# First expert stage with its weight parts, ranks and counts in other places, and attention's output projection as three products of high and low parts

## What is computed

```python
x = x + 0.5 * _L0_ffn_ref(_layernorm(x), gate_up_proj, down_proj, router_w)
x = x + _L0_attn_ref(_layernorm(x), conv_w, conv_b, wq, bq, ..., wo, bo, proj_w, proj_b)
x = x + 0.5 * _L0_ffn_ref(_layernorm(x), gate_up_proj, down_proj, router_w)
```

```python
out = mha_out @ proj_w + proj_b      # proj_w is 64 x 256
```

## Time and profile before

| | us |
|---|---|
| median of 3 runs | 794.87 |
| lowest and highest | 792.56 and 800.15 |
| the profiled execution's own time | 796.36 |
| its span in the trace | 794.6 |
| PE busy | 690.0 (87%) |
| DVE busy | 528.2 (66%) |
| ACT busy | 490.2 (62%) |
| POOL busy | 335.8 (42%) |

### The profile page before, as it was taken

How to read it: one execution, slowest core, us unless ns; L and a number is a source line. 1 busy time by engine, 2 the same in 40 slices (tenths; PEclk the granted TensorE clock), 3 DMA queues, 4 the chain that set the end, 5 groups by cost and what they waited for, 6 DMA issues and landing times. The chain is left out here.

```text
span 794.6 us, 19426 instructions
## 1 busy us (share of the span) xinstructions
PE 690.0 (87%) x5468; PEld 603.7 (76%) x5468; DVE 528.2 (66%) x1813; ACT 490.2 (62%) x1734; POOL 335.8 (42%) x361
## 2 busy tenths in 40 slices
PE   3999799999999799998988889989635999999944
PEld 3976699999975688877767777778424999999833
DVE  6578566666656587786767576857664777777643
ACT  4766566666653587767766657767522666666633
POOL 5100544444416444455555545252551444444500
PEclk9999999999999999999999999999956999999979
DMA  9930354444422110011111111010124444444279
GB/s 313 279 110 13 124 147 141 143 130 127 128 82 85 39 41 28 28 41 55 55 55 48 61 41 48 22 55 2 61 91 117 132 128 125 128 131 126 83 288 346
DMA packets 57863, 83.40 MB, mean 105 GB/s; under 512 B 9520, under 2 KB 43827, under 8 KB 57780
## 3 DMA queue, kind: packets, MB, share of 16 engines
q1 hardware_dynamic: 44772, 47.63, 19.0%
q0 software_dynamic: 13008, 34.69, 14.0%
HBM read 45.77 MB, written 37.44 MB: 105 GB/s over the span
## 5 line engine op out<-in xcount | busy, mean ns | idle before, releaser
L1539 PE MATMUL CC<-w_hi,turned_parts 128*128 x568 | 172.5, 345 | 0.3 <-DVE turned_parts L1161 0.2
L655 POOL DMA_INDIRECT shared<-h_rows,tok_i x71 | 67.3, 948 | 119.0 <-issue 58.7
L667 POOL DMA_INDIRECT y_rows<-shared,y_dest x71 | 69.9, 985 | 88.7 <-DVE y_dest L1173 74.9
L683 POOL TENSOR_TENSOR pr<-pr,prec 128x1024 f32<-128x1024 f32 x31 | 58.8, 1895 | 112.2 <-DVE prec L1353 110.9
L1539 PEld LDWEIGHTS CC<-w_hi,turned_parts 128*128 128x128 f32 x568 | 103.8, 190 | 1.0 <-issue 0.9
L1539 PE MATMUL CC<-w_lo,turned_parts 128*128 x284 | 91.8, 323 | 0.0
L729 ACT ACTIVATE shared<-CC 128x176 f32<-128x176 f32 x142 | 45.1, 317 | 75.1 <-PE CC L1539 72.6
L813 ACT ACTIVATE pr<-SS,nmax 128x128 f32<-128x128 f32 x256 | 90.4, 400 | 0.8 <-issue 0.8
L700 POOL DMA_INDIRECT h_regions<-h_store,dest x64 | 63.1, 987 | 47.3 <-DVE dest L1256 27.3
L1156 DVE TENSOR_TENSOR shared<-shared,CC 128x176 f32<-128x176 f32 x142 | 48.0, 338 | 51.6 <-ACT shared L729 30.0
L691 POOL DMA_INDIRECT yg<-y_rows,slot_i x64 | 62.6, 977 | 34.9 <-DMA y_rows<-shared 15.5
(11 more groups left out here) (318 smaller groups left out, 2055.4 us busy)
## 6 DMA issues: line engine op xcount, KB each, us to landing
shared<-h_regions SPq DMA_DIRECT2D x71, 129.0 KB
y_rows<-shared SPq DMA_DIRECT2D x71, 128.0 KB
w_lo<-y_rows SPq DMA_DIRECT2D x9, 512.0 KB, 8.4
x_sb<-in_x_dram SPq DMA_DIRECT2D x8, 512.0 KB, 8.3
out_dram<-x_sb SPq DMA_DIRECT2D x16, 256.0 KB, 5.7
w_hi<-y_rows SPq DMA_DIRECT2D x7, 512.0 KB, 11.9
w_lo<-in_gupT_dram SPq DMA_DIRECT2D x2, 1408.0 KB, 10.7
h_regions<-pad_rows SPq DMA_DIRECT2D x15, 129.0 KB
```

The costliest lines, as they stand in the source:

```text
L655: pool.indirect_dma_start(out=rows[:, s % RING, 0:D], out_offset=None, in_=h_dram[:, :], in_offset=bass.IndirectOffsetOnAxis(ap=tok_i[:, s ...
L667: pool.indirect_dma_start(out=y_dram[0:TOPK * TOKENS, :], out_offset=bass.IndirectOffsetOnAxis(ap=y_dest[:, s:s + 1], axis=0), in_=y_sb[:, ...
L683: pool.tensor_tensor(pr[:, q, :, :], pr[:, q, :, :], prec[:, q, :].unsqueeze(2).to_broadcast([P, NH, P]), ALU.mult).then_inc(t["norm"], 1)
L1539: i = pe.matmul(CC[:, 512 * (u % 2):512 * (u % 2) + GU], rows_part[:, u % 2, c * P:(c + 1) * P], weights, start=(n == 1), stop=(n == 3 * DC))
```

## The change

In the first stage:
- POOL mends the roots of the first three groups ahead of the constants, not of two; DVE's own constants come behind all five groups of statistics.
- The ranks of the third group come after tile 29, not 31; those of the fourth and the counts come directly behind `low_parts(0)`.
- ACT writes one of an expert's two high parts behind each tile from 22 on (`HIGH_FROM`), so that five experts are done by tile 31; the other three come behind `lows(0)`, `lows(1)` and `lows(2)`, and `attention_weights` behind the last of these.
- `PE_LOW` is 6: PE makes six experts' low parts, DVE two, and DVE makes them after the tables, not before. Two tiles' lane instructions of DVE move from ahead of the fourth group's places to behind the first three groups of one-hot tiles.

In attention mhaT becomes a high part and a low part in fp32r (in the memory of `minus_ident` and `ones_r`), proj_w too (`proj_hi` in `projb_parts`, `proj_lo`), and `project` is three fp32r matmuls. proj_w is loaded behind conv_w into memory of `tile_oh`.

The second reads the first's result, so it waits for it. The diff, cut to what matters:

```diff
@@ -55,12 +55,12 @@
 LEAD = 4
-RANKS_AFTER = {15: 0, 20: 1, 31: 2}
+RANKS_AFTER = {15: 0, 20: 1, 29: 2}
+HIGH_FROM = 22
 HALF_WAY = TOKENS // 2
 CHUNKS = TILES // CHUNK
-WEIGHTS_AFTER = {22: 0, 25: 1, 28: 2, 30: 3}
-PE_LOW = 7
+PE_LOW = 6
 LOW_PIECES = 3
@@ -136,7 +136,7 @@
         mha_bias = sb("mha_bias", [P, 1])
-        proj_sb = sb("proj_sb", [P, D])
+        proj_lo = sb("proj_lo", [P, D], F32R)
         projb_sb = sb("projb_sb", [33, D])
@@ -265,7 +265,8 @@
         prec = sb("prec", [P, 2, NH])
-        mhaT = tile_oh[:, :, :].rearrange("p j n -> p (j n)").bitcast(F32)[:, 2 * P:3 * P]
+        mhaT_hi, mhaT_lo, proj_hi = minus_ident, ones_r, projb_parts
+        proj_sb = tile_oh[:, :, :].rearrange("p j n -> p (j n)").bitcast(F32)[:, 1536 + G_USED:1536 + G_USED + D]
         eps = sb("eps", [P, 1])
@@ -347,7 +348,7 @@
                  (bqk_sb[:, 1, :], bk.rearrange("a (m p) -> p (a m)", p=P)), (wvT_sb[:, :, :], wvT),
-                 (wo_sb[:, :, :], wo), (bo_sb[:, :], bo), (proj_sb[0:W, :], proj_w), (proj_sb[W:2 * W, :], proj_w),
+                 (wo_sb[:, :, :], wo), (bo_sb[:, :], bo),
                  (projb_sb[0:1, :], proj_b), (projb_sb[32:33, :], proj_b)]
@@ -566,6 +567,8 @@
             sp.dma_start(conv_sb, conv_w).then_inc(loaded, 16)
+            for half in range(2):
+                sp.dma_start(proj_sb[W * half:W * (half + 1), :], proj_w).then_inc(loaded, 16)
             store_y(0)
@@ -705,9 +708,9 @@
             stats_of = list(enumerate(STATS))
-            correct_roots(stats_of[0:2])
+            correct_roots(stats_of[0:3])
             other_constants()
-            correct_roots(stats_of[2:])
+            correct_roots(stats_of[3:])
             warm_up()
@@ -833,12 +836,13 @@
                 a.preload_act_table_set("natural_log_exp_and_others")
-                a.wait_ge(loaded, 16 * (len(loads) + 1))
+                a.wait_ge(loaded, 16 * (len(loads) + 3))
                 a.activation(conv_qk[0][:, :, :], conv_sb_qk, ACT.Copy).then_inc(wprep, 1)
                 a.wait_ge(projb, 4)
+                a.activation(proj_hi[:, :], proj_sb[:, :], ACT.Copy).then_inc(wprep, 1)
                 a.activation(projb_all[:, 0:D], G[:, 0:D], ACT.Copy).then_inc(projb, 1)
@@ -866,9 +870,9 @@
-                def weights(e):
+                def weights(e, of=slice(0, 2)):
                     a.wait_ge(w_in[e // (E // 2)], 16 * len(w_loads[0]))
-                    for whole, hi, _ in weight_parts(e):
+                    for whole, hi, _ in list(weight_parts(e))[of]:
                         a.activation(hi, whole, ACT.Copy).then_inc(high, 1)
@@ -884,8 +888,9 @@
                         norm(t + LEAD)
-                    if t in WEIGHTS_AFTER:
-                        weights(WEIGHTS_AFTER[t])
+                    if t >= HIGH_FROM:
+                        n = t - HIGH_FROM
+                        weights(n // 2, slice(n % 2, n % 2 + 1))
@@ -893,13 +898,13 @@
-                for e in range(4):
+                for e in range(PE_LOW):
                     lows(e)
-                    weights(e + 4)
-                a.wait_ge(loaded, 16 * len(loads))
-                attention_weights()
-                for e in range(4, PE_LOW):
-                    lows(e)
+                    if e < 3:
+                        weights(e + 5)
+                    if e == 2:
+                        a.wait_ge(loaded, 16 * len(loads))
+                        attention_weights()
@@ -1069,11 +1074,9 @@
                 r = R[0]
-                for c in range(4):
+                for c in range(len(STATS)):
                     first_stats(c)
                 constants()
-                for c in range(4, len(STATS)):
-                    first_stats(c)
                 first_pick(0)
@@ -1087,20 +1090,19 @@
                 v.tensor_tensor(wtmp[:, 1, :], best[:, :, 1], best[:, :, 0], ALU.subtract).then_inc(r["diff"], 1)
-                first_lanes(2, GROUP // 2, GROUP)
+                first_lanes(2, GROUP // 2, 3 * GROUP // 4)
                 first_places(3)
                     first_tiles(g)
+                first_lanes(2, 3 * GROUP // 4, GROUP)
                 first_lanes(3, 0, GROUP)
                 v.tensor_reduce(expert_at[:, :], passed_tile[:, :], AX.X, ALU.add).then_inc(first["experts"], 1)
-                for e in range(PE_LOW, E):
-                    low_part(e)
                 v.wait_ge(first["table"], 1)
@@ -1110,6 +1112,8 @@
                 v.tensor_tensor(mha_bias[0:W, :], G[0:W, W:W + 1], bo_sb[:, :], ALU.add).then_inc(wprep, 1)
+                for e in range(PE_LOW, E):
+                    low_part(e)
                 v.scalar_tensor_tensor(out=slot_i[:, :, :], in0=stile_h[:, :, :], scalar=float(P), in1=slane[:, :, :],
@@ -1339,8 +1343,10 @@
                         v.wait_ge(t["mha"], i)
-                        v.tensor_tensor(mhaT[:, :], F[:, 0:P], mha_bias[:, 0:1].to_broadcast([P, P]), ALU.add
-                                        ).then_inc(t["mhaT"], 1)
+                        step(v.tensor_tensor(mhaT_hi[:, :], F[:, 0:P], mha_bias[:, 0:1].to_broadcast([P, P]), ALU.add))
+                        v.scalar_tensor_tensor(out=mhaT_lo[:, :], in0=F[:, 0:P], scalar=mha_bias[:, 0:1],
+                                               in1=mhaT_hi[:, :].bitcast(F32), op0=ALU.add, op1=ALU.subtract
+                                               ).then_inc(t["mhaT"], 1)
                     if there(i + 3) and i >= 0:
@@ -1395,6 +1401,9 @@
                                     conv_v_parts[0][:, c, :, :].bitcast(F32), ALU.subtract).then_inc(wprep, 1)
+                v.wait_ge(wprep, 7 + 2 * (1 + DC) + 1)
+                v.tensor_tensor(proj_lo[:, :], proj_sb[:, :], proj_hi[:, :].bitcast(F32), ALU.subtract
+                                ).then_inc(wprep, 1)
                 turns(turn)
@@ -1587,8 +1596,10 @@
                     pe.wait_ge(t["mhaT"], b + 1)
-                    pe.matmul(G[:, 0:D], mhaT[:, :], proj_sb[:, :], start=False, stop=True, skip_group_check=True
-                              ).then_inc(t["out"], 1)
+                    for n, (part, weights) in enumerate(((mhaT_hi, proj_hi), (mhaT_hi, proj_lo), (mhaT_lo, proj_hi))):
+                        x = pe.matmul(G[:, 0:D], part[:, :], weights[:, :], start=False, stop=(n == 2),
+                                      skip_group_check=True)
+                    x.then_inc(t["out"], 1)
@@ -1728,21 +1739,20 @@
             low_parts(0)
+            first_ranks(GROUPS - 1)
+            first_counts()
             low_parts(1)
-            first_ranks(GROUPS - 1)
             low_parts(2)
-            first_counts()
-            low_parts(3)
             pe.wait_ge(loaded, 16 * len(loads))
             weights_vo()
-            low_parts(4)
+            low_parts(3)
             bias_vo()
                 first_table(g)
-            low_parts(5)
+            low_parts(4)
             first_table(GROUPS - 1)
             turn_experts()
-            low_parts(6)
+            low_parts(5)
             pe.wait_ge(low_act, LOW_PIECES * PE_LOW)
@@ -1753,7 +1763,7 @@
             keep_clock(F[:, :], 44)
-            pe.wait_ge(wprep, 7 + 2 * (1 + DC))
+            pe.wait_ge(wprep, 7 + 2 * (1 + DC) + 2)
             attention()
```

## The result

| | before | after |
|---|---|---|
| median of all runs, us | 796.73 (4 runs, 792.56 to 800.15) | 811.68 (4 runs, 805.18 to 814.47) |
| ratio, 95% interval | | 1.0157 (1.0112 to 1.0201) |
| profiled execution, us; its span | 796.36; 794.6 | 805.18; 803.4 |

The forecast was 793.8 us, range 786 to 801. The time lies 11 us above the range. The change is slower by 15 us, and the interval of the ratio leaves out 1. (The profiled execution of after is the fastest of its four, so its trace shows 9 of the 15 us.)

The account below looks back on a forecast made before the run. TensorE was taken to bound attention and pace router and experts, with a cross-engine chain up to tok_i between. First stage -3.6 and attention +2.5 give -1.1 us: 795.3 from the profiled 796.36, 793.8 in medians; range 786 to 801.

Parts of the forecast that it names:

- Roots earlier, router 0.83 us: First stage, tile 8: GpSimd's third-group roots ahead of its constants shorten TensorE's stall, so the router gains 0.83 us.
- High parts spread, gain 0.4 us; ranks at tile 29: First stage: spreading ACT's high parts gains 0.4 us (0 to 0.9); third-group ranks come two turns, 2.35 us, earlier.
- Idle time of about 1 us ahead of the counts, low part 1 near 57.7, clock rises: First stage: PE idles about 1 us between ranks and counts, reaches the second low part near 57.7; clock rise given 0.6.
- Table's last piece 3.4 us earlier: First stage: with one low part fewer and ranks and counts already paid, PE reaches the table's last piece 3.4 us earlier.
- covered by 0.8 us, and not a cost: First stage: DVE's two low parts behind tok_i end 0.8 us before PE's first expert transposes, so they cost nothing.
- the expert stage is PE-paced at a constant pitch and passes the shift on: Expert stage: a microsecond earlier at tok_i is a microsecond earlier for everything behind it.
- Attention +2.5 us, bounds -8 to +10.6: Attention's projection: PE saves 0.16 us a block, DVE's second mhaT instruction delays L1699; 2.5 us slower, 8 faster to 10.6 slower.
- PE idle before the F matmul in over 14 turns, and longer: Attention, sign of being right: TensorE waits before L1699 in more than the earlier 14 turns, and longer.
- The other 18 have something in hand ... with the others at zero: Attention: the 18 turns where PE did not wait, -2.9 to +3.1 us together, were counted as zero.
- mhaT's second instruction becomes the bound: Attention rival, DVE L1342 to PE L1699 every turn: 0.33 x 32 = 10.6 us, time 801.9; chance 0.12.
- experts starting after 80.5: First stage's end, sign of being wrong: the expert stage starts after 80.5 us; the forecast had first transposes near 78.
- attention longer by over 6 us: Attention, sign of being wrong: the stage lengthens by over 6 us, where 2.5 us was forecast.

Follow-up runs that it names:

- e1: Kernel before with only the change's first-stage edits, attention as before: 757.73 us, ratio 0.9996, where the kernel before takes 757 us.
- e4: Kernel before with only the first-stage edits, VectorE's four low-part subtractions put back ahead of its wait for the last table: 755.39 us, ratio 0.9971.
- e2: Kernel before with only the projection's edits, first stage as before: 761.19 us, ratio 1.0048, where the kernel before takes 757 us.
- e7: Kernel before plus a second VectorE operation between mhaT and its signal, writing a tile nobody reads: 799.47 us, ratio 1.0102.
- e14: Kernel before with only the projection's edits, on a chip with late signals (kernel before 796 and 797 us): 809.04 us, ratio 1.0157.
- e13: Kernel before with only the first-stage edits, on a chip with late signals (kernel before 796 and 797 us): 794.38 us, ratio 0.9973.
- e5: The whole changed kernel run again beside the kernel before, on a chip where that takes 792 us: 800.03 us, ratio 1.0093.
- e12: The whole changed kernel run again, on a chip where the kernel before takes 796 and 797 us: 807.69 us, ratio 1.0138.
- e6: Changed kernel without mhaT's second VectorE operation, the third projection matmul reading the high part again: 790.45 us, ratio 0.9976 to the kernel before.
- e11: Kernel before with only first-stage edits, low-part subtractions ahead of the last table's wait, on a chip with late signals: 794.00 us, ratio 0.9973.

## Why the prediction was wrong

By its own steps:

1. *Roots earlier, router 0.83 us:* right; the stall at tile 8 is gone, and it was worth 0.98 us (2.16 less 1.18).
2. *High parts spread, gain 0.4 us; ranks at tile 29:* the second right, the first wrong. Before, two tiles took 1.63 and 1.62 us in place of 1.17; now three do (1.32, 1.54 and 1.54), so 0.9 us are lost as before. With step 1 the errors partly cancel: the first low part starts at 51.56 ("near 51.3"), the third ranks at 48.06 ("near 48").
3. *Idle time of about 1 us ahead of the counts, low part 1 near 57.7, clock rises:* right but for 0.3 us; 0.86 us, 58.03, 0.75 us for the matmul of 480 columns.
4. *Table's last piece 3.4 us earlier:* it was 2.7. The way from low part 1 to it is 3.1 us shorter (15.2 for 18.3), and low part 1 itself starts 0.4 later than before.
5. **The step that failed first:** "They end some 4.6 us after the table piece starts ... covered by 0.8 us, and not a cost", of VectorE's low parts. They did end in time (77.88, 4.63 after 73.25). But the cover was reckoned for VectorE alone: what ran beside them was GpSimd's gather, on which all waited, and it could not go on until they had ended. e1 against e4 is the price: 2.3 us of the 3.6. A second premise failed by less: "the expert stage is PE-paced at a constant pitch and passes the shift on". From the first transposes to the `keep_clock` matmuls e1 and e4 take 0.8 and 1.0 us more than e2, with the longer time at the lower clock. The rise of the clock behind the ranks was weighed, its fall at the experts' start was not.
6. *Attention +2.5 us, bounds -8 to +10.6:* the mechanism (mhaT's second operation against L1699) was the right one, and the sign "PE idle before the F matmul in over 14 turns, and longer" came (18 turns, 24.6 us). On chip A the term is 3.0 us in the stretch and 4.0 in the median. That it came so near 2.5 is luck: TensorE saves 0.08 us a block, not 0.16, and the wait in the fullest turn of four grows by 0.85 us, not by 0.17 to 0.33, because VectorE, and not TensorE, is the bound of that turn, and its row carries two of the operations.
7. **The step that failed most:** the size on a chip like the one measured. "The other 18 have something in hand ... with the others at zero" took the waits of the earlier trace rows as fixed and only added to them. On the chips where TensorE's signals are late, the one operation, 0.35 us long, cost 7.6 us (e7) and the projection 11.9 us (e14), above the rival's 0.33 x 32 = 10.6. From e13 to e14 TensorE's wait before F grew by 7.3 us and VectorE's waits for late signals by 12.5; how the two make 11.9 is not shown. The rival "mhaT's second instruction becomes the bound", at 0.12, was what happened, in place and in kind: 801.9 by its own sum, and 805.5 with the first stage's gain taken as nothing. The measured 811.7 is more than that. The loss of the same kernel was 15 us in the first runs, 8.2 on B (e5) and 10.6 on C (e12). Of the prediction's own signs of being wrong two came: experts starting after 80.5 (80.72), and attention longer by over 6 us (6.7).

The chances were too sure: "DVE is busy 0.3 us more per turn, which it can bear at 46 of 60" is an average over turns that differ. In one of four it had nothing to spare (chip A).

No version with the projection in parts beat the kernel before, but for e6, which computes another sum. The first-stage edits with the low parts ahead of the table are 0.3% below the kernel before on A (e4, 0.9971, 0.9959 to 0.9982) and about as much on C (e11), where the interval reaches 1.

## What to carry to other kernels

Cover for an operation moved off the chain must be asked of every engine that runs beside it: four VectorE subtractions, in a gap in which nothing waited for VectorE, held up the GpSimd gather on which all waited. And an engine's average load says nothing of the turn in which it is the bound: find the fullest turn in the timeline and price an added operation there, as often as it occurs in that row. Before a gain of under 1% is claimed or denied, measure on more than one chip.

## What the runs showed that was not expected

*Signals of TensorE that come late on some chips.* ScalarE's copy of the transposes and VectorE's sum, e1 on chip A, then the kernel before in the first trace:

```profile
382.83 1.10 PE L1629 MATMUL CC<-ident,pr 128*128 128x128 f32 x8
...
384.56 0.68 PE L1590 MATMUL G<-proj_sb,tile_oh 128*128 128x256 f32 x2
...
383.96 1.08 ACT L804 ACTIVATE shared<-CC 128x512 f32<-128x512 f32 x2 [1.18 <-PE CC L1629]
...
385.28 0.42 DVE L1327 TENSOR_TENSOR x_sb<-x_sb,G 128x256 f32<-128x256 f32 x1 [1.11 <-PE G L1590]
```

```profile
396.89 1.09 PE L1629 MATMUL CC<-ident,pr 128*128 128x128 f32 x8
...
398.62 0.68 PE L1590 MATMUL G<-proj_sb,tile_oh 128*128 128x256 f32 x2
...
399.55 1.08 ACT L804 ACTIVATE shared<-CC 128x512 f32<-128x512 f32 x2 [2.27 <-remote]
...
401.78 0.42 DVE L1327 TENSOR_TENSOR x_sb<-x_sb,G 128x256 f32<-128x256 f32 x1 [3.19 <-remote]
```

On chip A ScalarE starts 0.03 us behind the transposes' modelled end, and VectorE's sum 0.72 behind the projection's start. In the other trace it is 1.57 and 3.16 us, at the same matmul starts and a granted clock of 1.00. In the 29 turns of e1 for which the trace has all eight transposes, the first number was never over 0.04. The kernel before takes 757 us on the one chip and 792 to 797 on the others, and most of that lies in attention (stretch 267.4 in e1, which has the old projection, 299.4 us in the first trace). What is waited for at L1327 is the projection's signal from TensorE, so remote stands for that here; why it comes late is open.

*VectorE and GpSimd stop each other,* three times with numbers: the gather 3.87 for 0.95 us beside two-input subtractions, a cast 1.05 for 0.22 us beside GpSimd's product, a two-element operation 0.42 for 0.16 us beside GpSimd's subtraction. In none of the three does a wait show it; the duration does.
